# A decoder layer in one kernel: the first tile normed by itself, V's first weights loaded early, tiles turned one by one inside V's products

## The reference

```
x = x + attention(layernorm(x))      # 16 heads of 128, causal, tanh soft cap, one sigmoid gate per head
x = x + token_experts(layernorm(x))  # 4 experts chosen by token id, silu(x A^T) * (x A^T) through A, A of 512 x 512
x = x + moe(layernorm(x))            # router with top 2 of 8 experts (352 wide) plus a shared expert (704 wide)
```

```
layernorm(x) = (x - mean(x)) / sqrt(var(x) + 1e-5)
qkv = layernorm(x) @ w_qkv           # 512 x 6144
```

## Time and profile before

| | |
|---|---|
| median of 3 runs | 1588.45 us (1587.54 to 1589.22) |
| the profiled execution, its own time | 1586.04 us |
| its span | 1584.3 us |
| TensorE's mean granted clock | 0.997 |
| PE busy | 1556.4 us, 98% of the span |
| PE weight loads busy | 1332.5 us, 84% |
| DVE busy | 1040.2 us, 66% |
| ACT busy | 583.0 us, 37% |
| POOL busy | 447.3 us, 28% |

### The profile page before, as it was taken

One profiled execution on the slowest core, in us unless ns is written; L12 is line 12 of the kernel. 1 busy time (PEld: TensorE's weight loads), 2 busy tenths in 40 slices (PEclk: granted clock), 3 DMA queues, 4 the chain that ended last, 5 costly groups with the idle time before them and its releaser, 6 DMA issues.

```text
span 1584.3 us, 23799 instructions
## 1 busy us (share of the span) xinstructions
PE 1556.4 (98%) x7776; PEld 1332.5 (84%) x7777; DVE 1040.2 (66%) x2230; ACT 583.0 (37%) x997; POOL 447.3 (28%) x378
## 2 busy tenths in 40 slices
PE   7999999999999999999999999999999999999996
PEld 6888888888888888888888887888888889999995
DVE  4898887788877788887787778655663572222221
ACT  4454443444444334344334334333111323233232
POOL 4445332234223234222233221103200003333342
PEclk9999999999999999999999999999999999999998
DMA  8786664677876786875686776466631036778743
GB/s 297 281 306 230 229 213 150 235 279 275 303 269 228 258 304 251 302 293 220 243 313 249 295 298 257 140 202 206 231 100 47 7 123 210 234 195 270 208 86 40
DMA packets 105812, 351.70 MB, mean 222 GB/s; under 512 B 11056, under 2 KB 31536, under 8 KB 100208
## 3 DMA queue, kind: packets, MB, share of 16 engines
q1 hardware_dynamic: 92688, 312.63, 54.7%
q0 software_dynamic: 13024, 37.79, 10.2%
HBM read 227.18 MB, written 123.19 MB: 221 GB/s over the span
## 4 chain that ended last, share of the span: by engine, by line
PE 93%; DVE 4%; DMA 1%; POOL 1%; issue 1%; ACT 1%; POOLq 0%; SPq 0%; ACTq 0%; DVEq 0%
PE bank L366 30%; PE bank L368 30%; PE bank L367 29%; PE bank L1946 1%; PE bank L2067 1%; POOL store L660 0%; DMA rows<-x_rows,ids_e 0%; DMA wv_raw<-wv_in 0%; PE bank L2024 0%; DMA out<-x_early,ids_e 0%; DVE place_hot L1628 0%; DVE tile_vals L1638 0%; DVE resid L1272 0%; DVE resid L1464 0%; PE bank L1746 0%
## 5 line engine op out<-in xcount | busy, mean ns | idle before, releaser
L701 POOL TENSOR_TENSOR probs<-probs,causal 128x256 f32<-128x256 f32 x126 | 90.2, 737 | 409.9 <-ACT probs L879 409.9
L368 PE MATMUL bank<-store,wqk 128*128 128x512 f32 x512 | 202.1, 395 | 0.0
L367 PE MATMUL bank<-store,wqk 128*128 128x512 f32 x512 | 201.8, 394 | 0.0
L366 PE MATMUL bank<-store,wqk 128*128 128x512 f32 x512 | 201.7, 394 | 0.0
L1272 DVE SCALAR_TENSOR_TENSOR resid<-bank,factor,resid 128x512 f32<-128x512 f32 x256 | 189.2, 741 | 1.3 <-PE bank L368 1.1
L660 POOL TENSOR_TENSOR pre_split<-pre_raw,pre_split 128x1528 fp32r<-128x1528 f32 x34 | 120.3, 3539 | 141.5 <-ACT pre_split L841 141.5
L877 ACT ACTIVATE probs<-bank 128x512 f32<-128x512 f32 x189 | 85.9, 529 | 131.3 <-PE bank L368 131.3
L368 PEld LDWEIGHTS bank<-store,wqk 128*128 128x128 f32 x512 | 96.0, 188 | 22.8
L367 PEld LDWEIGHTS bank<-store,wqk 128*128 128x128 f32 x512 | 96.1, 188 | 20.8
L366 PEld LDWEIGHTS bank<-store,wqk 128*128 128x128 f32 x512 | 96.0, 188 | 19.8
L1303 DVE TRANSPOSE_TENSOR_REDUCE bank<-probs 128x16 f32<-128x512 f32 (+3 forms) x256 | 108.4, 491 | 0.0
(11 more groups left out here) (333 smaller groups left out, 3920.3 us busy)
## 6 DMA issues: line engine op xcount, KB each, us to landing
pre_parts<-pre_split SPq DMA_DIRECT2D x34, 1528.0 KB, 6.5
wqk<-wqk_parts SPq DMA_DIRECT2D x96, 512.0 KB, 3.6
pre_raw<-pre SPq DMA_DIRECT2D x34, 764.0 KB, 7.8
store<-wv_parts SPq DMA_DIRECT2D x12, 2048.0 KB, 9.0
wo<-wo_parts SPq DMA_DIRECT2D x48, 512.0 KB, 6.8
expert_w<-pre_parts SPq DMA_DIRECT2D x8, 2816.0 KB, 11.7
wqk_parts<-wqk SPq DMA_DIRECT2D x16, 1024.0 KB, 5.1
expert_w<-pre_parts SPq DMA_DIRECT2D x8, 1536.0 KB
```

The costliest lines, as they stand in the source:

```text
L366: nc.tensor.matmul(out_ap, a_hi, b_hi, start=first, stop=False)
L367: nc.tensor.matmul(out_ap, a_hi, b_lo, start=False, stop=False)
L368: return nc.tensor.matmul(out_ap, a_lo, b_hi, start=False, stop=last)
L701: nc.gpsimd.tensor_tensor(diagonal, diagonal, causal[:, :, :], ALU.mult).then_inc(S["masked"], 1)
```

## The change

The first norm group becomes tile 0 alone and the second tiles 1 to 3. The load of V's first quarter moves ahead of the load of x's third tile (`load_x(2)`). POOL waits for the first apply before its first low part. PE turns only tile 0 before the products, and tile n + 1 within product n; before, it turned tiles 0 and 1 first and tile n + 2 within product n. On ACT the copy of tile 1 moves behind all high parts of V's weights, and on DVE the low part of V's third quarter moves ahead of the applies of tiles 2 and 3.

```diff
-        FIRST_GROUPS = ((0, 2), (2, 4))
+        FIRST_GROUPS = ((0, 1), (1, 4))
...
-            for i in range(TB):
+            def load_x(i):
                 sp.dma_start(resid[:, i, :], xv[:, i, :]).then_inc(S[f"x_tile{i}"], 16)
-            for k in range(KC):
+
+            def load_first_v(k):
                 sp.dma_start(wv_raw[:, k, :], wv_in[0][:, k, :]).then_inc(S[f"wv_first{k}"], 16)
+
+            load_x(0)
+            load_x(1)
+            load_first_v(0)
+            load_x(2)
+            load_x(3)
+            for k in range(1, KC):
+                load_first_v(k)
...
             rsqrt(0, *FIRST_GROUPS[0])
+            pool.wait_ge(S["xn_ready"], 1)
             low_v(0, 0)
             rsqrt(1, *FIRST_GROUPS[1])
...
             high_v(0, 0)
             xnT_high(0, FIRST_BANKS[0])
             high_v(0, 1)
-            xnT_high(1, FIRST_BANKS[1])
             high_v(0, 2)
             high_v(0, 3)
+            xnT_high(1, FIRST_BANKS[1])
             xnT_high(2, FIRST_BANKS[2])
             v_high(0, 0)
             xnT_high(3, FIRST_BANKS[3])
...
             first_stats(0)
+            first_eps(0)
             first_stats(1)
-            first_eps(0)
+            ln_apply(0, 0, xn[:, 0, :], "xn_ready")
             first_stats(2)
-            ln_apply(0, 0, xn[:, 0, :], "xn_ready")
-            ln_apply(0, 1, xn[:, 1, :], "xn_ready")
             first_stats(3)
             first_eps(1)
             xnT_low(0, FIRST_BANKS[0])
+            ln_apply(1, 1, xn[:, 1, :], "xn_ready")
+            low_v(0, 2)
             ln_apply(1, 2, xn[:, 2, :], "xn_ready")
             ln_apply(1, 3, xn[:, 3, :], "xn_ready")
-            low_v(0, 2)
             xnT_low(1, FIRST_BANKS[1])
             xnT_low(2, FIRST_BANKS[2])
             v_low(0, 0)
...
             transpose_xn(0, FIRST_BANKS[0])
-            transpose_xn(1, FIRST_BANKS[1])
             for n in range(TB):
                 pe.wait_ge(S["xnT_lo_done"], n + 1)
                 if n >= 2:
                     pe.wait_ge(S["v_lo_done"], n - 1)
-                v_product(n, bank[n % 2], (lambda: transpose_xn(n + 2, FIRST_BANKS[n + 2])) if n + 2 < TB else None)
+                v_product(n, bank[n % 2], (lambda: transpose_xn(n + 1, FIRST_BANKS[n + 1])) if n + 1 < TB else None)
```

## The result

| | median us (lowest to highest) | runs |
|---|---|---|
| before | 1587.81 (1585.41 to 1591.05) | 19 |
| changed | 1589.71 (1588.65 to 1592.16) | 19 |

The ratio is 1.0014, with a 95% interval of 1.0008 to 1.0020: 1.3 to 3.2 us slower. That is less than the 0.2% that a measurement of this kernel can call, but the interval leaves out 1. The profiled execution of the changed kernel took 1589.58 us, with a span of 1587.8 (3.5 more than before).

What follows compares the result with a forecast made beforehand. TensorE, holding 93% of the chain, was taken as the bound. 1.5 us won up to product 1 and 3.0 lost behind it made 1.5 us later, so 1589.9 us against the median of 1588.45; range 1587.0 to 1591.6.

Steps and rivals of the forecast that it cites:

- The waits behind product 1: Before products 2 and 3: PE waits 0.77 and 1.70 us for bank copies queued behind other copies.
- A: Rival at products 2 and 3: no waits, product 3 at 21.3, a gain of 1.0 us, 1587.5 us; chance 0.12.
- C: Rival: the wait before product 3 drops TensorE to 1.2 GHz, 1591.7 us, slower by over 0.2%; chance 0.05.
- my sum: Main forecast: product 1 at 14.8, product 3 at 23.7 against 22.24, 1.5 us later, 1589.9 us; chance 0.62.
- B: Rival at the loads: x's last tile lands at 8.6, product 1 at 15.6, product 3 2.3 late, 1590.8 us; chance 0.10.
- D: Rival: clock rises at 15.4 as before, product 1 at 15.7, 2.4 late, 1590.9 us; chance 0.11.
- The head: Stage up to product 1's start: earlier first apply and transposes, product 1 at 14.8 against 16.28, 1.5 us won.
- The clock: In product 0: TensorE rises to 2.4 GHz 3.6 us after PE's last stop, at 13.4.
- GpSimd's added wait: GpSimd's wait for the first apply, at 6.26, before its first low part: costs nothing.
- The rule on shared ports: DVE beside GpSimd: two-SBUF-input instructions also wait; V's third quarter ends 13.1 instead of 12.0, product 1 unmoved.
- Behind the stage: After product 3's start: its shift is carried whole to the kernel's end; the weights' reload stays covered by 3.4 us.

Runs made afterwards that it cites:

- v0_first: The changed kernel with ACT and DVE copying product 0's bank ahead of tile 2's copies; ratio to before 1.0009 (1.0000 to 1.0018).
- v1_first: The changed kernel with ACT and DVE copying product 1's bank ahead of tile 3's copies; ratio to before 1.0009 (1.0000 to 1.0018).
- both_first: The changed kernel with both reorderings, v0_first's and v1_first's, at once; ratio to before 1.0004 (0.9995 to 1.0013).
- turn_ahead: The changed kernel with tiles 1 and 2 turned inside product 0 and tile 3 inside product 1; ratio to before 0.9996 (0.9987 to 1.0005).
- after_again: The changed kernel measured once more, unchanged, as a control for its scatter; ratio to before 1.0018 (1.0009 to 1.0027).
- turn_ahead_loads_back: turn_ahead with before's load order, no POOL wait for the first apply, rsqrt(1) and ACT's tile 0 copy moved ahead; ratio to before 1.0002 (0.9993 to 1.0011).
- before_again: The kernel before the change measured once more, unchanged, as a control; ratio to before 1.0001 (0.9991 to 1.0010).
- no_pool_wait: The changed kernel without POOL's added wait for the first apply; ratio to before 1.0016 (1.0007 to 1.0025).
- alone_and_pair: turn_ahead with groups 0, 1, 2-3, V's second quarter loaded earlier, tile 1's rsqrt and tile 0's low part moved ahead; 1585.61 us, ratio to before 0.9984.
- loads_back: The changed kernel with before's load order, four tiles of x and then V's quarters; ratio to before 1.0019 (1.0010 to 1.0028).

## Why the prediction was right, and where it wasn't

The call (no change that a measurement can tell, a point 1.5 us above before) held: 1.9 us by the medians, 1.3 to 3.2 by the interval. The waits behind product 1 stand in every case but A, and they were found, without C's fall of the clock. Between my sum, B and D the time doesn't decide: they have 1.5, 2.3 and 2.4 us, all within the interval. By the head, the first profile (product 1 at 15.08) fits my sum and the mean of six (15.90) fits B or D. That the point came so near is in part luck: the gain that it takes off for the head doesn't show on average. (The range's high end is also mis-added: 1590.9 and half a microsecond are 1591.4, not 1591.6.) Step by step:

**The waits behind product 1** were right in place, releaser and nearly in size. Product 1's group starts at 16.58 and product 2 goes on 2.69 later (forecast 2.64); product 2's group starts at 20.73 and product 3 goes on 3.62 later (3.57). What the sum missed is small: a half product took 1.50 and 1.46 instead of 1.36, since the first matmul behind a stop or a seam is followed 0.3 us later and not 0.23. So 8.93 became 9.27. v0_first, v1_first and both_first show these waits by taking them away; turn_ahead shows that what makes them is turning tile n + 1 only within product n.

**The head** was the mis-sized term. In the profiled execution the first apply (5.51) and the transposes (6.20) were as early as said, and product 1 started at 15.08 against a forecast of 14.8. Two sizes inside were off in opposite directions: x's last tile landed at 7.1, not 7.8, and V's second quarter late enough for a stop of 0.44 us. (GpSimd's power of three columns took 0.87, where the sum had 0.65, but the low part behind it waited for ACT's high part until 9.62.) They cancel: product 0's third quarter starts at 13.32, the very time of the sum, and the 0.28 us behind that are the clock, which rose at 13.8 and not at 13.4. This profile has the earliest product 1 of the six. Also, "product 1 can start at 14.8, against 16.28" set a scattering start against one profile of before. Over six profiles of this head product 1 averages 15.90, and over two of before 16.01. So the 1.5 us credited were 0.1 on average. My bounds for the tile's landing, 6.2 to 7.8 from one row each, should have been 7.1 to 9.1. That is rival B's mechanism in part: B had the tile at 8.6 and product 1 at 15.6, and the means are 8.1 and 15.90. By these averages product 3 is 3.2 us late, twice what I forecast and at the interval's upper end, while the medians differ by 1.9 us, in after_again's series by 2.3. Both profiles of before are of executions 1.8 and 1.0 us faster than their medians, so their landmarks may be early ones; where the rest of the difference lies is open.

**The clock.** I let it rise 3.6 us after PE's last stop. In the changed kernel it rose at 13.8, 2.6 behind the stop that ended at 11.17; in turn_ahead_loads_back at 16.9, 5.7 us after PE had begun to run closed. The same program rose at 13.8 and again at about 15.0 (the changed kernel, after_again), and at 15.4 and 14.5 (before, before_again). D was therefore a matter of chance in each execution, not a case of its own. C is refuted: the 1.59 us stop of the changed kernel is followed by matmuls 0.31 and then 0.23 us apart. That the moment of the rise varies from run to run, as the Trainium skill has it (TensorE: Matmul & The Clock Gate, "What's actually happening"), agrees with these traces.

**A** is refuted by the trace: product 3 starts 9.27 us behind product 1, where A had 6.46. **GpSimd's added wait** costs nothing, as said (no_pool_wait).

**The rule on shared ports** was one of the two sentences on the Trainium skill (SBUF — State Buffer, "Who interferes with whom"), and the runs show what before didn't: V's third quarter on DVE, with two operands from SBUF, took 1.31 us beside POOL's low parts in the changed kernel, against 0.68 alone in the earlier trace rows. The trace agrees with it. As forecast, that moved nothing.

**Behind the stage** the shift was carried whole up to 225 us, 2.2 us there. Near 228 us it falls to 1.9. The two spans differ by 3.5 us, so 1.3 us come later: the distance between the two traces goes from 1.9 to 2.7 us at one place near 655 us, where PE of the changed kernel waits for a reload of Q and K's weights, and to 3.3 us near 1030 us. before_again moves against before at the first place too, by 0.6 us, so such a step needs no change of the program, and after_again has no such wait. v0_first shows the same wait with another length (its waits of PE, 200 to 700 us: us in total, times, longest):

```profile
PE bank L366 <- DMA wqk<-wqk_parts: 1.2, 1, 1.2
```

Why that transfer lands late in some executions, and what lies behind the step near 1030 us, was not looked into.

## What to carry to other kernels

Where a result bank is reused two products later, look at what each copying engine has queued ahead of that bank's copy: three other copies stood ahead of it on ACT before the change too, with 1.1 us to spare. The first of them needs the turned tile, so turning the tile one product later made all of them late and PE stood still for 1.6 us, with no work added. A group of its own for the first tile isn't enough to start the first product early: in the changed kernel the tile's low part stood on DVE behind the stats and eps of the tile that lands last. alone_and_pair takes it ahead of them and starts product 0 before that tile lands. And take the landing of the first loads from several executions: it moved by 2 us here, more than any gain or wait in the sum.

## What was unexpected in the hardware

- TensorE's half-speed stretch at the start is not in the granted clock, which reads 1.00, but in the spacing (0.43 against 0.23 us for 512 columns, 1.2 and 2.4 GHz). It ended at about 13.8 us in the changed kernel and 15.0 in after_again, 14.5 in before_again, 15.4 in before, 16.4 in loads_back and 16.9 in turn_ahead_loads_back. In the last, the window 11.20 to 17.00 shows PE closed (5.80 busy) and, ahead of the DMA share and the GB/s, a granted clock of 1.00, though the matmuls were 0.43 apart up to 15.93:

```profile
11.20:17.00 5.80, 5.80 (x17) 4.19 (x18) 3.92 (x4) 0.82 (x2) 2.95 (x2) 1.00 0.60 242
```

- GpSimd's power of a column of 128 numbers takes 0.58 us for one column, 0.72 for two and 0.87 for three: some 0.15 us for each further column. In alone_and_pair two columns took 0.92 beside DVE's apply and its low part of V's third quarter.
- The same 256 KB load, fifth in the queue, took 4.4 to 6.4 us from issue to landing in six executions of one head.
